# Position blocks added by accumulating transposes, and six product banks in three stages

## The reference

```
scores = q k^T / 4 + (positions taken from rel_pos_emb, one value per query, key and head)
attention = softmax(causal(scores)) v
```

## Time and profile before

| | |
|---|---|
| runs, median (lowest to highest) | 2950.18 us (2942.37 to 2951.38) |
| profiled execution | 2953.07 us, span 2951.8 us |
| granted TensorE clock, mean of the span | 0.915 of full speed |
| TensorE matmul busy | 2516.5 us, 85% of the span |
| VectorE / ScalarE / GpSimd busy | 1221.9 / 871.9 / 571.0 us |

### The profile page before, as it was taken

One profiled execution on the slowest core, in us unless ns is written; L12 is line 12 of the kernel. 1 busy time (PEld: TensorE's weight loads), 2 busy tenths in 40 slices (PEclk: granted clock), 3 DMA queues, 4 the chain that ended last, 5 costly groups with the idle time before them and its releaser, 6 DMA issues.

```text
span 2951.8 us, 34531 instructions
## 1 busy us (share of the span) xinstructions
PE 2516.5 (85%) x13798; PEld 1740.3 (59%) x13798; DVE 1221.9 (41%) x2235; ACT 871.9 (30%) x2379; POOL 571.0 (19%) x566
## 2 busy tenths in 40 slices
PE   3875999994899497887899999599956999877999
PEld 3764777763677363422466667477742788733555
DVE  6454111118488664455333321300034355655220
ACT  1110111113376161355322221122214345313220
POOL 2431222214200101211344310222220100012000
PEclk8976999996899798999899999699977999988999
DMA  4003444423001000300000000322227323100000
GB/s 149 1 29 139 148 173 156 146 77 103 0 2 48 0 2 0 119 0 22 8 1 0 1 1 0 123 83 85 80 84 322 154 88 129 37 25 0 8 8 15
DMA packets 73752, 189.50 MB, mean 64 GB/s; under 512 B 9551, under 2 KB 52950, under 8 KB 65655
## 3 DMA queue, kind: packets, MB, share of 16 engines
q1 hardware_dynamic: 65590, 169.11, 15.9%
q0 software_dynamic: 8000, 18.18, 2.0%
HBM read 143.88 MB, written 46.09 MB: 64 GB/s over the span
## 4 chain that ended last, share of the span: by engine, by line
PE 47%; DVE 6%; DMA 2%; ACT 1%; POOL 1%; issue 1%; SPq 0%; POOLq 0%; DVEq 0%; ACTq 0%
PE psum L221 25%; PE psum L3140 6%; PE psum L1685 3%; PE psum L2183 2%; PE psum L3149 2%; PE psum L2170 2%; PE psum L1680 2%; DMA positions<-arena 1%; PE psum L1696 1%; DVE stats L253 1%; PE psum L1711 1%; DVE arena L2230 1%; PE psum L2400 1%; POOL small L2598 1%; PE psum L404 1%
## 5 line engine op out<-in xcount | busy, mean ns | idle before, releaser
L221 PE MATMUL psum<-arena 128*128 128x256 f32 (+6 forms) x4112 | 995.2, 401 | 24.9 <-DVE arena L3236 13.1
L221 PEld LDWEIGHTS psum<-arena 128*128 128x128 f32 (+3 forms) x4112 | 719.0, 182 | 289.4 <-issue 148.6
L1770 DVE TENSOR_REDUCE small<-psum 128x4 f32<-128x1024 f32 (+1 forms) x112 | 137.0, 1224 | 158.7 <-PE psum L1685 110.9
L263 POOL TENSOR_SCALAR x_moments<-x_moments 128x4 f32<-128x4 f32 x48 | 12.0, 251 | 957.0 <-DVE x_moments L256 956.5
L1326 DVE TENSOR_TENSOR arena<-arena,psum 128x256 f32<-128x256 f32 x138 | 58.0, 420 | 318.0 <-ACT arena L1298 316.7
L1176 POOL DMA_INDIRECT l_out<-arena,slot_tables x86 | 85.7, 996 | 495.8 <-ACT arena L1304 288.0
L3140 PE MATMUL psum<-arena 128*128 128x512 bf16 x768 | 166.4, 379 | 0.0
L1745 ACT ACTIVATE arena<-psum,small 128x128 f32<-128x128 f32 (+1 forms) x384 | 149.3, 417 | 49.2 <-DVE small L1770 49.2
L1781 DVE COPY arena<-psum 128x512 f32<-128x512 f32 x224 | 143.7, 682 | 1.8 <-PE psum L1696 1.5
L404 PE MATMUL psum<-ident,z 128*128 128x128 f32 x256 | 47.6, 345 | 109.7 <-DVE z L274 79.6
L1745 ACT ACTIVATE z<-psum,small 128x128 f32<-128x128 f32 (+1 forms) x256 | 104.0, 426 | 119.0 <-DVE small L1770 118.9
(11 more groups left out here) (332 smaller groups left out, 3555.0 us busy)
## 6 DMA issues: line engine op xcount, KB each, us to landing
arena<-L_ffn_w_in SPq DMA_DIRECT2D x23, 2176.0 KB, 9.0
arena<-L_ffn_W_in SPq DMA_DIRECT2D x16, 1024.0 KB
positions<-arena SPq DMA_DIRECT2D x16, 1024.0 KB, 6.0
arena<-positions SPq DMA_DIRECT2D x16, 1024.0 KB, 8.2
arena<-l_out SPq DMA_DIRECT2D x16, 512.0 KB, 8.1
positions<-arena SPq DMA_DIRECT2D x16, 512.0 KB, 6.6
arena<-positions SPq DMA_DIRECT2D x16, 512.0 KB, 9.0
l_out<-arena SPq DMA_DIRECT2D x2, 2048.0 KB, 14.1
```

Of the source, the lines that this page charges most:

```text
L221: last = nc.tensor.matmul(out, lhsT, rhs, start=(n == 0), stop=(n == len(pairs) - 1))
L1770: nc.vector.reduce_max(self.minus_top(h), use.bank(u).rearrange("p (h l) -> p h l", l=L), AX_X, negate=True).then_inc(self.topped.up(), 1)
```

## The change

The matmuls that add the blocks of positions (L1685) get the transpose mode, still with `start=False`: a transpose that accumulates in the bank. And three stages hand out six banks for their products, 0 to 5, and leave banks 6 and 7 to the turning of z.

```
--- before.py
+++ after.py
@@ class L0Autocorrelation
-        u = self.uses = Uses(k)
+        u = self.uses = Uses(k, count=6)
@@ Attention.pe_score
-                    mm = nc.tensor.matmul(bank[:, at + P * a:at + P * a + P], self.positions(t, a, head), k.ident, start=False,
+                    mm = nc.tensor.matmul(bank[:, at + P * a:at + P * a + P], self.positions(t, a, head), k.ident, is_transpose=True, start=False,
                                           stop=True, skip_group_check=True)
```

## The result

The changed kernel took 2906.49 us in the median of four runs (2903.45 to 2907.74) where the kernel before took 2950.78 (2942.37 to 2953.57): a ratio of 0.985, with a 95% interval of 0.9837 to 0.9864, or 44.3 us less. Measured again beside its parts it took 2902.9 against 2948.88 (ratio 0.9842, 0.9828 to 0.9855), 46.0 us less. Forecast were 8.6 us less. The profiled execution has a span of 2904.8 us.

A forecast was written before the change was run, and what follows sets the result against it. The prediction took TensorE as the bound, busy all 217.30 us of the attention with positions. Position blocks -3.6 and banks -5.0 made -8.6 us, taking the median from 2950.18 to 2941.6, range 2932 to 2952.

The forecast's parts named there:

- The step that failed: Position blocks at L1685: 768 matmuls become transposes, 16 per unit taking 1.81 us instead of 1.88; 3.6 us saved.
- the banks: Six banks: in `L1Attention` pair 6 no longer waits, moments of group 3 come 5.0 us earlier; other two stages 0.
- The pace: L1685: 16 transposes behind the scores take 0.93 + 0.88 = 1.81 us, with weight loads of 140 ns.
- The bounds set for it: Position blocks at L1685: from no gain, 0 us, to a loss of 69 us at 203 ns per transpose.
- The covers: Attention with positions: VectorE and ScalarE, with over 40% of room, follow a TensorE 2% quicker; the next positions arrive in time.
- Rival 5: Position blocks: a transposed block takes a quarter of a plain one, 118 to 29 ns; 2877 us, chance 0.03.
- Rivals 1 and 2: Attention with positions: clock low longer at the start, 2946.6 us, chance 0.10; transposes don't hold the clock, about 3125, 0.03.
- Rival 3: Position blocks at L1685: accumulating costs a transpose extra, slower beyond 23 ns each, 3010 us at 203 ns; chance 0.05.
- rival 4: Whole change: only the banks count, 2945.2 us, chance 0.10; or only the positions, 2946.6 us, chance 0.07.

The follow-up runs named there:

- the positions alone: The kernel before with only the position blocks (L1685) made transposes, eight banks kept: 2905.11 us against 2952.32; beside the whole change, 2904.33 against 2902.9.
- the overwriting run: The changed kernel with start=True at L1685, so its transposes overwrite the bank: 2903.59 us against 2953.74 for the kernel before, ratio 0.9827.
- plain_turns: The kernel before with the eight transposes of exponentials per unit (L1696) made plain f32 products: 3058.39 us against 2953.74, ratio 1.0357.

## Why the prediction was wrong

**The step that failed** is the first of the change: "Nothing is added or moved: 768 matmuls become transposes with the same operands". It took the x768 of the trace for the number of blocks, and the x16 of a unit for sixteen blocks. The section on the kernel says the same ("16 blocks of positions in each, 768 in all"), and it gives eight matmuls to each pair of `Product` where the code has four, by the same mistake. A unit has eight blocks in the code: eight heads with one key tile, or four heads with two; that is 8 x 48 = 384. An f32 product of this shape is two instructions on TensorE, each with a weight load of its own, and a transpose is one. So the term "48 units x 0.075 = 3.6 us" compared 16 half products with 16 whole transposes. With eight it is 48 x (1.88 - 0.93) = 45.6 us, from rows that were on the table: 0.93 is the prediction's own reading of the earlier trace rows. Measured were 45.6 in the stage and, with the positions alone, 44.6 and 47.2 in the totals. The sum would have been -50.6, or 2899.6. The whole change measured 44.3 and 46.0 less, so this sum still misses by 4.6 to 6.3 us: about the term of the banks, which the totals of the whole don't show.

The error could have been seen without any new row. L1676 is two matmuls in the code and x2 in the trace, in bf16; L1680 in a unit with two key tiles is four products in f32, and x8; L1696 is eight transposes and x8. A comparison of one line's count with the loop that issues it gives the factor.

**The pace** of a transpose (0.93 us for eight behind the scores) and the weight load of 140 ns were right. That accumulation is free was an assumption that held, and the overwriting run shows it. The bounds set for it were of no use, for they were drawn around the price of one instruction and not around the number of them.

**The covers** held: VectorE and ScalarE followed a stage that is a fifth shorter, not 2%, and the positions arrived; TensorE was never idle in its 174 us.

**Rival 5** (a quarter, 2877) was nearest in kind: a transposed block is much cheaper than a plain one. It was given 0.03 because the rows at 118 and 110 ns seemed to exclude it. They exclude a factor between instructions, and say nothing of one between blocks. The Trainium skill's factor of four for f32, in the Terms of "TensorE: Matmul & The Clock Gate", points the right way and is too large by two for these 128x128 blocks: the measured factor is 1.88 / 0.93 = 2.0.

**Rivals 1 and 2** didn't come: the clock was low near the start for 6.8 us as before and at 1.00 in all of the stage that follows, with transposes in nearly half of TensorE's time (16 at L1685 and 16 at L1696, 3.7 us, in two units of 7.7 us). Part 4 of the same page of the Trainium skill says that transposes don't count as busy for the clock. The half of other matmuls keeps this stretch from testing that alone; the row that does, 16 transposes at 0.50 and a clock of 1.00 behind them, speaks against it. **Rival 3** is out by the overwriting run. Of **rival 4** the half with only the banks is out by the positions alone; the half with only the positions is out in the stage, by pairs of traces with a like clock, and not in the totals, where the whole and the positions alone are 1.4 us apart.

**The banks** were right for the trace that was read: the wait of pair 6, 1.9 us from copy to moments as in the other stage, 5.0 us at L2037, nothing in the other two stages. That the changed kernel's trace met the 5.0 so closely is in part luck with the clock: some 1.7 of it are the low clock of the wait, which didn't come in `positions_alone`, and four of the seven traces without the wait have lost 3.2 of their gain at L2037. The kernel with this edit alone measured 4.6 us faster, with an interval of 1.8 to 7.4.

## What to carry to other kernels

Before multiplying a duration by a count, hold the count of the trace against the loop in the code: one call in f32 may be two instructions, and an edit of its mode may remove one of them. An f32 product with the identity that only turns a block costs twice its transpose, also where it adds to a bank, and wherever TensorE is never idle the difference is the gain. A bank that a helper takes at a fixed place should not be one that the next product needs; moving the counter does as well as having fewer banks. What such a wait costs is partly the clock's doing, so one trace doesn't give its price.

## What the runs showed of the hardware

A transpose in f32 adds to what its bank holds at the pace at which it overwrites, 0.93 us for eight.

The clock can differ between executions at the same code. In the run with the counter moved on it fell behind the turning of group 2, where in the changed kernel it stayed up. Windows and eight transposes of the former:

```profile
969.90:983.00 13.10, 6.99 (x14) 2.74 (x12) 3.50 (x3) 2.74 (x5) 0.00 (x0) 0.50 0.00 0
```

```profile
972.95 1.94 PE L404 MATMUL psum<-ident,z 128*128 128x128 f32 x8 [1.75 <-ACT z L330]
```

And of the changed kernel:

```profile
969.00:981.50 12.50, 5.65 (x22) 2.61 (x20) 4.90 (x5) 3.73 (x7) 1.43 (x1) 1.00 0.00 0
```

```profile
975.28 1.06 PE L404 MATMUL psum<-ident,z 128*128 128x128 f32 x8 [1.75 <-ACT z L330]
```

The same transposes behind the same wait of 1.75 us take 0.9 us more, and the four matmuls behind them 1.8 more. Against the kernel before, matched instruction by instruction, that run had gained 5.0 us ahead of this point and 1.7 at L2037; 1.7 of the 3.2 lost came back by the end of `L1MixtureOfDepths`. It isn't the time saved that does this: the same fall stands in `plain_turns`, which saved nothing there, and is missing in three traces that saved the same 5.0 us. What decides it no run here shows. Two executions with the same code ahead of an edit stood up to 4 us apart before they reached it, so an effect of 5 us is read in its stage, in more than one trace, and needs many runs in the total.
